# Attention scores on eight tiles of the TensorE array and the Wv product on two, both in full fp32

## What is computed

```python
q = per_head_ln((ln(x) @ Wq).heads)           # 8 heads of 64, 32 queries per sequence
k, v = (context @ Wkv).heads                  # 257 keys per sequence; k = per_head_ln(k)
attn = einsum('bhnd,bhmd->bhnm', q, k) * 64**-0.5
attn = softmax(where(mask, attn, -inf), -1)
x = x + einsum('bhnm,bhmd->bhnd', attn, v) @ Wo
```

## Time and profile before

| | |
|---|---|
| time, median of 3 runs | 787.98 us (787.05 to 789.36) |
| the profiled execution | 791.38 us, its span 789.6 us |
| TensorE products, busy | 748.8 us, 95% of the span |
| VectorE / ScalarE / GpSimd, busy | 552.7 / 494.8 / 238.8 us |
| mean granted TensorE clock | 0.977 |

### The profile page before, as it was taken

How to read it: one execution, slowest core, us unless ns; L and a number is a source line. 1 busy time by engine, 2 the same in 40 slices (tenths; PEclk the granted TensorE clock), 3 DMA queues, 4 the chain that set the end, 5 groups by cost and what they waited for, 6 DMA issues and landing times.

```text
span 789.6 us, 13562 instructions
## 1 busy us (share of the span) xinstructions
PE 748.8 (95%) x4501; PEld 653.6 (83%) x4501; DVE 552.7 (70%) x1046; ACT 494.8 (63%) x1089; POOL 238.8 (30%) x182
## 2 busy tenths in 40 slices
PE   4898999999999999999999998999999958999996
PEld 3687899899999898998999997988788856877875
DVE  6877886776867868867868776885567754555573
ACT  4666786785867768767858666556465423655650
POOL 2562212121211212121212113842860002555545
PEclk9999999999999999999999999999999957999999
DMA  8841211212121211212121302661106472566658
GB/s 299 86 120 41 66 57 41 81 48 72 40 80 40 80 40 58 61 40 80 41 79 41 112 22 52 178 211 54 54 1 214 145 284 78 96 110 109 106 77 319
DMA packets 59671, 75.18 MB, mean 95 GB/s; under 512 B 8784, under 2 KB 33360, under 8 KB 59632
## 3 DMA queue, kind: packets, MB, share of 16 engines
q1 hardware_dynamic: 52032, 58.16, 24.8%
q0 software_dynamic: 4720, 11.27, 7.9%
q10 hardware_dynamic: 2880, 5.24, 1.8%
HBM read 54.75 MB, written 19.92 MB: 95 GB/s over the span
## 4 chain that ended last, share of the span: by engine, by line
PE 83%; DVE 7%; DMA 3%; ACT 3%; issue 2%; POOL 1%; SPq 0%; POOLq 0%; ACTq 0%; DVEq 0%
PE pK L32 38%; PE pV L32 14%; PE pP L32 11%; PE pS L32 6%; PE pT L1700 3%; PE pT L1519 3%; PE pP L1683 2%; DMA big<-x_rows,idx_x 1%; PE pT L1814 1%; DMA fin<-total 1%; PE pT L1499 1%; PE pS L1768 1%; DVE bst L976 1%; DMA total<-big,idx 1%; DVE head_mean L996 1%
## 5 line engine op out<-in xcount | busy, mean ns | idle before, releaser
L32 PE MATMUL pK<-parts 128*128 128x512 f32 x840 | 210.5, 398 | 0.7 <-POOL parts L547 0.7
L516 POOL TENSOR_TENSOR parts<-big,parts 128x1024 fp32r<-128x1024 f32 x32 | 77.3, 2416 | 338.8 <-ACT parts L741 338.8
L32 PEld LDWEIGHTS pK<-parts 128*128 128x128 f32 x840 | 152.3, 189 | 29.2 <-POOL parts L547 1.1
L32 PE MATMUL pK<-w,lhs 128*128 x276 | 71.5, 410 | 1.8 <-DVE lhs L1436 1.4
L32 PEld LDWEIGHTS pK<-w,lhs 128*128 128x128 f32 x276 | 51.9, 194 | 13.5 <-issue 3.5
L1018 DVE TENSOR_TENSOR kn<-pK,head_rs 128x512 f32<-128x512 f32 x62 | 42.6, 688 | 20.1 <-ACT head_rs L643 19.5
L1452 DVE TENSOR_TENSOR w_p<-big,w_p 128x1024 fp32r<-128x1024 f32 x22 | 27.0, 1226 | 39.5 <-ACT w_p L933 39.5
L769 ACT ACTIVATE pT<-pP 128x512 fp32r<-128x512 f32 x32 | 19.1, 598 | 55.6 <-PE pP L1683 55.6
L32 PE MATMUL pS<-kT,qblk 128*128 128x258 f32 x384 | 51.4, 284 | 2.0 <-DVE qoT L1052 2.0
L32 PE MATMUL pP<-pT,parts 128*128 128x256 f32 x384 | 53.0, 288 | 0.0
L32 PEld LDWEIGHTS pP<-pT,parts 128*128 128x128 f32 x384 | 47.6, 192 | 3.5
(11 more groups left out here) (320 smaller groups left out, 1638.2 us busy)
## 6 DMA issues: line engine op xcount, KB each, us to landing
big<-in_ctx_dram SPq DMA_DIRECT2D x32, 512.0 KB, 3.8
total<-zero SPq DMA_DIRECT2D x32, 256.0 KB, 4.0
w_raw<-in_L_ffn_w_dram SPq DMA_DIRECT2D x16, 512.0 KB, 5.6
big<-in_L_ffn_w_dram SPq DMA_DIRECT2D x8, 512.0 KB, 7.6
fin<-total SPq DMA_DIRECT2D x8, 512.0 KB, 7.2
big<-in_L_xattn_Wkv_dram SPq DMA_DIRECT2D x2, 1024.0 KB, 11.0
x_rows<-big ACTq DMA_DIRECT2D x8, 256.0 KB, 2.1
total<-big ACTq DMA_DIRECT2D x8, 256.0 KB, 2.4
```

The lines of the kernel that those rows point to most:

```text
L32: last = pe.matmul(out, lhs(a, c), rhs(b, c), start=start and c == first and n == 0, stop=stop and c == chunks - 1 and n == 2)
L516: nc.gpsimd.tensor_tensor(ctxN[:, u, LO], ctx_raw[:, u], ctxN[:, u, HI].bitcast(F32), ALU.subtract).then_inc(cn_lo, 1)
```

## The change

- Scores: 8 full fp32 products in place of 12 split ones. Head e of chunk c uses the array tile of 64 rows by 32 columns at (64 e, 32 c): 64 rows of the query copy `q_b` against 257 keys of `kT`, to 32 partitions of `pS`. `qblk` with its zeros is gone; GpSimd copies a sequence's queries (`queries`).
- Keys and weighted context are kept once, as fp32 (`kT`, `z`), with one copy on ScalarE and one on VectorE in place of two HI and two LO steps.
- Wv: for each chunk and head 5 fp32 products (4 chunks of the width and the leftover row) on the array tile of 128 rows by 64 columns at (0, 64 e), 128 columns each, only the head's own rows: 40 products for 52. The result has one bank, and `out_copy` is one step. Wv is loaded to its place and not split.
- The last context rows are multiplied in fp32 with Wk and with Wv (4 products each); the one with Wv is moved ahead of the first scores.
- Waits: an empty instruction (`nop`) takes the waits ahead of each tiled block. SyncE waits for the Wk product of the last rows before it loads Wo, and ScalarE's copy of the context waits for the weighted context of two sequences before.

```diff
@@ TensorE: batch, scores
-                    pe.wait_ge(k_lo, b * MT)
-                    pe.wait_ge(qb_lo, b * 2)
+                    pe.wait_ge(kT0_set, b)
+                    pe.wait_ge(kT1_set, b)
                     pe.wait_ge(k_rem, b)
-                    for g in range(G):
-                        for j in range(2):
-                            c = 2 * g + j
-                            qb = lambda s, _: qblk[:, 1 - u, s, g, j * HD:j * HD + P]
-                            last = split_products(pe, pS[:, g, 0:M + 1], qb, lambda s, _: kT[:, s, c, :], 1,
-                                                  start=j == 0, stop=j == 1)
+                    pe.wait_ge(q_set, b)
+                    if not first:
+                        pe.wait_ge(sc_m, b - 1)
+                    pe.nop(nofuse=True)
+                    for c in range(C):
+                        for e in range(2):
+                            half = slice(e * HD, (e + 1) * HD)
+                            last = pe.matmul(pS[c * S:(c + 1) * S, e, 0:M], q_b[half, 1 - u, c, :],
+                                             kT[half, c, :], start=True, stop=True, tile_position=(e * HD, c * S))
@@ TensorE: out_tile
-                pe.wait_ge(pc_lo, (t + 1) * BT * 2)
+                pe.wait_ge(z0_set, (t + 1) * BT)
+                pe.wait_ge(z1_set, (t + 1) * BT)
+                pe.wait_ge(p_rx, (t + 1) * BT)
+                pe.nop(nofuse=True)
                 for c in range(C):
-                    o = (pV1[:, :], pP_flat)[c // 2][:, (c % 2) * 2 * P:(c % 2 + 1) * 2 * P]
-                    split_products(pe, o, lambda s, k: wkv[:, s, k, D + c * P:D + (c + 1) * P],
-                                   lambda s, k: z_p[:, s, k, c * 2 * P:(c + 1) * 2 * P], C, stop=False)
-                    if c == 0:
-                        pe.wait_ge(p_rx, (t + 1) * BT)
-                    last = pe.matmul(o, vrem[0:3 * B, c * P:(c + 1) * P], ...)
+                    for k in range(C + 1):
+                        for e in range(2):
+                            o = pV1[e * HD:(e + 1) * HD, c * P:(c + 1) * P]
+                            cols = slice(c * P + e * HD, c * P + (e + 1) * HD)
+                            weights, rows = (wv[:, k, cols], z[:, k]) if k < C else (vrem[0:3 * B, cols], rem_b[0:3 * B])
+                            last = pe.matmul(o, weights, rows[:, e * C + c].rearrange("p b q -> p (b q)"), start=k == 0,
+                                             stop=k == C, tile_position=(0, e * HD))
@@ TensorE: after the last query turn of the head (was in the first batch)
+            pe.wait_ge(*raw_in("xv"))
+            for c in range(C):
+                last = pe.matmul(pV1[:, :], remT[:, c, :], wv[:, c], start=c == 0, stop=c == C - 1)
+            last.then_inc(rem_pe, 1)
@@ TensorE: head, t == 5
-                    split_products(pe, pV1[:, :], lambda s, c: remT[:, s, c, :], wk, C).then_inc(rem_pe, 1)
+                    for c in range(C):
+                        last = pe.matmul(pV1[:, :], remT[:, c, :], raw("xk")[:, c], start=c == 0, stop=c == C - 1)
@@ VectorE: one step of keys, of the weighted context and of the output
+            def keys_copy(n):
+                dve.wait_ge(k_t, n * MT)
+                ts(kT[:, :, P:MT * P], pTT[1][:, :, :], 1.0, None, ALU.mult).then_inc(kT1_set, 1)
-                if nxt:
-                    query_low(b + 1, 1 - u)
+                    dve.wait_ge(pc_mm, p * 2 + 2)
+                    ts(z[:, 0:2, :, pr, :], prob_ctx(0), 1.0, None, ALU.mult).then_inc(z0_set, 1)
+                dve.wait_ge(o_mm, t + 1)
+                ts(qoT[:, :, bass.ds(t * P, P)], pV1[:, :].rearrange("p (c n) -> p c n", c=C), 1.0, None,
+                   ALU.mult).then_inc(o_out, 1)
@@ ScalarE
+            def keys_copy(n):
+                act.wait_ge(k_t, (n - 1) * MT + 1)
+                act.activation(kT[:, :, 0:P], pTT[0][:, :, :], ACT.Copy).then_inc(kT0_set, 1)
+                    if not first:
+                        act.wait_ge(pc_mm, (b - 1) * 2)
                     act.activation(ctxN[:, u, HI], ctx_raw[:, u], ACT.Copy).then_inc(cn_hi, 1)
-                    query_high(b + 1, 1 - u)
+                    act.activation(z[:, 2:4, :, pr, :], prob_ctx(1), ACT.Copy).then_inc(z1_set, 1)
@@ GpSimd: no low parts of Wv; ahead of ctx_parts(b, u) in the loop
+            def queries(b, u, used=True):
+                if used:
+                    pool.wait_ge(sc_mm, b - 1)
+                nc.gpsimd.tensor_copy(q_b[:, u], qoT[:, :, bass.ds(b * S, S)]).then_inc(q_set, 1)
@@ SyncE
-            load_weight("xv", "xq")
+            sp.wait_ge(*raw_in("xq"))
+            sp.dma_start(wv, jobs["xv"][0]).then_inc(raw_in("xv")[0], 16)
...
+            sp.wait_ge(rem_pe, 2)
             load_weight("xo", "xk")
```

More of the change, by code:

```diff
@@ L254, in perceiver_block @@
         XO_ORDER = (3, 0, 1, 2)
-        high_count = lambda name, c: JOBS.index(name) * 4 + (XO_ORDER.index(c) if name == "xo" else c) + 1
+        SPLIT = tuple(n for n in JOBS if n != "xv")
+        high_count = lambda name, c: SPLIT.index(name) * 4 + (XO_ORDER.index(c) if name == "xo" else c) + 1
         w_sum = sem("w_sum")
@@ L517, in ctx_parts @@
                                         ALU.subtract).then_inc(cn_lo, 1)
+            def queries(b, u, used=True):
+                if used:
+                    pool.wait_ge(sc_mm, b - 1)
+                nc.gpsimd.tensor_copy(q_b[:, u], qoT[:, :, bass.ds(b * S, S)]).then_inc(q_set, 1)
             ctx_parts(0, 0)
-            low_part("xv", (2, 3))
+            pool.wait_ge(q_out, 1)
+            for b in range(2):
+                queries(b, b, used=False)
             ctx_parts(1, 1)
@@ L540, in _ @@
                     b = k * 2 + u
+                    queries(b, u)
                     ctx_parts(b, u)
-            ctx_parts(B - 2, 0)
-            ctx_parts(B - 1, 1)
+            for b in (B - 2, B - 1):
+                queries(b, b % 2)
+                ctx_parts(b, b % 2)
             def out_low(t):
@@ L723, in _ @@
                     act.activation(head_rs[:, 2], head_log[:, 2], ACT.Exp, scale=-0.5).then_inc(k_rs, 1)
-                if t == 6:
-                    query_high(1, 1)
                 if t == TILES - 1:
-                    high_part("xv", (C - 1,))
                     act.wait_ge(rem_pe, 3)
[L729 to L732, removed]
+                    act.activation(kT_rem[:, :, :], pAV[0][:, :, 0:B], ACT.Copy).then_inc(rem_act, 1)
+                    keys_copy(1)
             k_square(1, 0)
@@ L777, in batch @@
                 if main:
-                    for t in range(MT):
-                        act.wait_ge(k_t, b * MT + t + 1)
-                        act.activation(kT[:, HI, :, t * P:(t + 1) * P], pTT[t][:, :, :], ACT.Copy).then_inc(k_hi, 1)
+                    keys_copy(b + 1)
                 if nxt:
@@ L1660, in batch @@
                     k_half(b, 1, u)
-                if first:
-                    pe.wait_ge(w_lo[JOB["xv"]], C)
-                    split_products(pe, pV1[:, :], lambda s, c: remT[:, s, c, :], weight(wkv, D, 2 * D), C).then_inc(rem_pe, 1)
                 if r == 1 and not first:
@@ L1710, in batch @@
                                 if first:
-                                    pe.wait_ge(rem_dve, 5)
-                                elif r == 0:
-                                    pe.wait_ge(p_rl, tile)
+                                    pe.wait_ge(rem_act, 6)
+                                else:
+                                    pe.wait_ge(z0_set, b - 1)
+                                    if r == 0:
+                                        pe.wait_ge(p_rh, tile)
+                                    if r == 1:
+                                        pe.wait_ge(o_out, tile)
                             last = split_products(pe, o, lambda s, t: ctxN[:, 1 - u, s, t, c * P:(c + 1) * P],
```

148 lines of the change are left out of this document (43 added, 105 removed).

## The result

The changed kernel takes 753.5 us (median; 753.1 to 754.65) where the kernel before takes 788.31 (787.05 to 789.36) on the same chip. Measured again beside later kernels it gave 0.957 (0.955 to 0.959), 754.85 us.

What follows compares the result with a forecast made beforehand. The prediction took TensorE's stream to bound the loop over sequences. Scores 0, Wv -11.0 and head -1.5 made -12.5 us, from the median of 787.98 to 775 us, with a range from 760 to 812.

Steps and rivals of the forecast that it cites:

- The bound: Loop over sequences, 90 to 470 us: TensorE busy 380.00 us of 380.00 at clock 1.00, so its stream sets the span.
- Free overlap: Score and Wv tiles work at once, each with its own work queued; 775 us, range 760 to 788, chance 0.45.
- program order: Rival: products start in program order, so a waiting tile holds back others; scores 2.34 us a block, 804 us, chance 0.30.
- the third case's term: Score block, each tile with work queued: issuing up to the last pair takes 0.60 us, block about 1.05 us.
- The bound of -0.4 a block: Score blocks: one end of the range -0.4 to +0.3 us a block around a gain of nothing.
- The passage: Going into and out of the tiled form at each tiled block: 0.4 us taken, bounds 0 and 0.71.
- Wv: Eight Wv blocks: 40 fp32 products on two overlapping tiles, 4.84 us for 6.21, a gain of 11 us in all.
- The head: Before the loop: last context rows multiplied in fp32 with Wk and Wv, low halves gone; sum -1.5 us.
- The step of 0.69 at 34.04: VectorE's low-part step before the Wk product of the last context rows, on the path; removal counted as -0.7 us.
- The relief: Steps VectorE and ScalarE lose per sequence, beside TensorE: counted as nothing while they stay ahead.
- The sum: Whole kernel: scores 0, Wv -11.0, head -1.5, together -12.5 us; from the median, 775 us.
- no overlap: Rival: tiles share what reads the moving data, all pairs run in turn; scores 3.86 us a block, 888 us, chance 0.10.

Runs made afterwards that it cites:

- the adjacent form: Changed kernel with each score product issued twice, back to back on its own tile: 770.05 us, ratio 0.977.
- the whole-array runs: Changed kernel with the score products, or in another run the Wv products, each taking the whole array instead of a tile: 840.02 us and 787.87 us.
- that load: Changed kernel with the removed VectorE and ScalarE work put back as unread steps, VectorE's reading SBUF twice: 811.01 us, ratio 1.028.
- the load that read PSUM: Changed kernel with the removed work put back, its 128x512 steps reading PSUM ahead of the copies: 765.93 us, ratio 0.970.

## Why the prediction was wrong, point by point

- **The bound** held: TensorE's stream at a clock of 1.00, so what is saved there ends sooner.
- **Free overlap against program order** was decided rightly, for the reason given: the engine hands work on before the earlier work is out. What the rival called program order is an order for each tile. The Trainium skill, "TensorE: Matmul & The Clock Gate", Part 3, says products start and end in program order; across tiles these traces contradict it for the starts, with second passes of early tiles 0.24 us behind the first pass of late ones, and in the adjacent form the second product of the program behind the fifteenth. The Trainium skill, "TensorEngine Tiling (Array Packing)", section Tiling Modes, says that tiles multiply in parallel, and that is borne out (0.60 for 3.47).
- **The failed step** is the third case's term 15 x 0.04 = 0.60 us for issue, in the scores. The 0.04 came from bf16 pairs with 128-column weights. It is a distance between starts on one whole array, where each product follows a load of its own. I read it as the price of issue, while on tiles eight products start within 0.06 us. Without this term the block is 2 x 0.216 = 0.43 plus the passage. With the 0.4 that I took for the passage it is 0.83, and the distance between blocks shows 1.45 - 0.68 = 0.77. So scores gave 0.68 x 32 = 21.8 us where the sum had 0: this is nearly all of the miss of 22.3. The bound of -0.4 a block was taken from the same term and was no bound. Why bf16 pairs stand 0.040 apart on the whole array was not tested.
- **The passage**, taken at 0.4 from tails and a load, measured 0.3 to 0.35. The distances agree: 0.77 - 0.43 = 0.34 for scores, and 4.75 - 4.44 = 0.31 for Wv.
- **Wv**: forecast 4.84 and -1.4 a block. The block takes 4.54, and in the mean a sequence with Wv exceeds one without by 4.75 (6.19 before): -1.44 x 8 = -11.5 for -11.0. This term was right.
- **The head**: forecast -1.5. The first scores start 1.87 later (forecast 1.3), and 2.79 go in the first sequence: -0.9. The step of 0.69 at 34.04 brought nothing: the Wk product starts at the same time without it (41.98 for 42.02).
- **The relief**, "worth nothing" as long as the other engines stay ahead: in the kernel as changed they do, and the 0.45 us of slack stayed 0.45. The sum needed no term for it. But the forecast didn't ask how much load would still fit at the new pace, and its argument that both ends are counted from the scores' end leaves out the mask step's queue. With a load like the removed one, 11 of the 34.8 us are not reached.
- **The sum** up to the end of the last Wv block, 472.53 for 507.97, is -35.4 in the profiled executions. The parts make -35.6: -21.8, -11.5 and -0.9, and -1.4 by luck of this pair of profiles. Behind a wait in the last but one sequence (at 479.44) TensorE's granted clock is 0.54 from 480 to 483 before, and 1.00 after at the same place. There the kernel before takes 5.28 us from the keys' transposes to the last scores, and the kernel after 3.92. In the second profile of the changed kernel, where the clock fell to 0.50, it is 5.42.
- **The rivals**: no overlap would have made 888, program order 804; the whole-array runs show what the first is made of. None of them ended on the gain's far side: a rival in which the tiles start together, at 2 x 0.216 and the passage, was missing. Its price would have been 775 - 20 = 755.

## What to carry to other kernels

Price tiled TensorE work by the fullest tile: its passes times the streaming time of one (0.216 us for 257 columns of fp32), plus about 0.3 us for each stretch of tiled work, and put no issue in turn on top as long as the order deals to the tiles in rotation. A run of ten passes for one tile ahead of the other cost 13 us here. When the bounding engine gets faster, look at what is queued on the others ahead of each hand-over, since a slack measured from the hand-over alone doesn't show that queue; and let a test load read what the real one reads and stand where it stood.

## What was unexpected in the hardware

- Tiles keep their own order: 16 pairs on eight tiles in 0.60 us, 32 in 1.03 and 1.08, with starts out of program order between tiles.
- How much is held for a busy tile is limited: in runs of ten pairs the other tile started when three were left (0.78 us a run; 0.55 and 1.11 were the ends).
- A passage into and out of tiles costs 0.3 to 0.35 us, and about half of it shows on the neighbours (transposes 0.85 and 1.02 for 0.79), so the block's own 0.60 flatters it.
- A VectorE step with both inputs in SBUF took 2.67 us for 0.68 beside a GpSimd step of 2.43. With the rest of that load it moved the end by 57 us; the load that read PSUM, and stood elsewhere in the queue, moved it by 11.
